# Local attention in pairs of 64 queries, values projected from the turned tokens, queries written three times and loaded in one transfer

## What is computed

```python
# allowed(i, j) = (j % 4 == 0) | (|i - j| <= 8);  16 heads of 8 features
x = x + 0.5 * ffn(layernorm(x))        # ffn: W_exp, butterfly, gelu, butterfly, W_con
x = x + attn(layernorm(x))
x = x + 0.5 * ffn(layernorm(x))

def attn(x):
    q, k, v = x @ q_w, x @ k_w, x @ v_w
    q = q * sigmoid(unity_scale)
    scores = where(allowed, q @ k.T / sqrt(8), -inf)
    return softmax(scores) @ v @ o_w + o_b
```

## Time and profile before

| | us |
|---|---|
| three runs | 346.88, 350.77, 351.96 |
| profiled execution, whole time | 348.5 |
| profiled execution, span from first to last instruction | 346.7 |
| PE busy | 278.6 |
| ACT busy | 201.4 |
| DVE busy | 160.1 |
| first score matmul | 114.5 |
| score matmuls of step 4 of the first unit | 128.0 |

### The profile page before, as it was taken

The page is one execution under the profiler, slowest core; times in us unless marked ns, Lnnn a source line. Parts: engine busy times, 40 slices in busy tenths (PEclk is TensorE's granted clock), DMA queues, the critical chain, the costliest instruction groups (busy, mean ns, idle before and its releaser), DMA issues.

```text
span 346.7 us, 5449 instructions
## 1 busy us (share of the span) xinstructions
PE 278.6 (80%) x2153; PEld 138.8 (40%) x2153; DVE 160.1 (46%) x421; ACT 201.4 (58%) x242; POOL 15.3 (4%) x15
## 2 busy tenths in 40 slices
PE   2299877893700429999899998999998999999995
PEld 0066673762400003233344434343443444347664
DVE  0799539899650001143425553255433544246410
ACT  1113335442410326799888998889998799952441
POOL 8000002102200000000000000000000000000000
PEclk9998989998565555899999999999999999999999
DMA  7900002326255530033312332123322300000111
GB/s 227 215 2 3 0 0 91 100 95 203 91 218 144 179 107 3 3 88 92 86 44 54 92 85 79 36 75 90 78 60 51 86 2 2 0 3 0 50 44 30
DMA packets 29242, 25.21 MB, mean 73 GB/s; under 512 B 4694, under 2 KB 25878, under 8 KB 29194
## 3 DMA queue, kind: packets, MB, share of 16 engines
q1 hardware_dynamic: 26501, 21.34, 22.1%
q10 hardware_dynamic: 2712, 3.49, 2.8%
HBM read 17.39 MB, written 7.63 MB: 72 GB/s over the span
## 4 chain that ended last, share of the span: by engine, by line
PE 68%; DVE 10%; SPq 9%; DMA 7%; ACT 2%; issue 1%; ACTq 1%; DVEq 0%
PE ps L585 19%; PE ps L566 18%; PE ps L459 8%; PE ps L418 6%; PE ps L572 5%; PE ps L595 5%; DMA k_strided<-k_strided_parts 3%; SPq L279 3%; PE ps L607 2%; DMA k_strided_parts<-probs_all 2%; DMA up_bias_sb<-L_ffn_up_bias 2%; DVE xnorm L822 2%; SPq L284 2%; PE ps L429 2%; SPq L307 2%
## 5 line engine op out<-in xcount | busy, mean ns | idle before, releaser
L762 ACT ACTIVATE probs_all<-ps 128x1024 f32<-128x1024 f32 x128 | 125.0, 1024 | 44.4 <-DMA q_parts<-probs_all 22.1
L566 PE MATMUL ps<-q_slots,k_strided 75*128 75x512 bf16 x256 | 74.0, 402 | 28.2 <-DMA v_local<-v_local_by_key 14.8
L585 PE MATMUL ps<-probs_all,v_strided 128*32 128x512 f32 x512 | 70.6, 625 | 0.0
L1019 DVE SCALAR_TENSOR_TENSOR probs_all<-probs_all,mask_k_sb 128x1024 f32<-128x1024 f32 x32 | 38.9, 1223 | 51.6 <-ACT probs_all L767 51.6
L566 PEld LDWEIGHTS ps<-q_slots,k_strided 75*128 75x128 bf16 x256 | 19.9, 100 | 86.3 <-ACT probs_all L762 28.5
L767 ACT ACTIVATE probs_all<-ps 128x1024 f32<-128x1024 f32 x32 | 32.7, 1021 | 9.2 <-PE ps L572 9.2
L691 ACT ACTIVATE gelu_h<-ps,bias_up 128x512 f32<-128x512 f32 x32 | 22.0, 687 | 24.7 <-PE ps L418 22.3
L418 PE MATMUL ps<-xnorm_t,up_folded 128*128 128x512 f32 x64 | 30.9, 627 | 3.4 <-ACT v_strided L717 1.9
L459 PE MATMUL ps<-down_folded,gelu_h 128*128 128x128 f32 x256 | 31.4, 283 | 2.1 <-ACT gelu_h L691 1.5
L459 PEld LDWEIGHTS ps<-down_folded,gelu_h 128*128 128x128 f32 x256 | 30.4, 198 | 3.6 <-ACT gelu_h L691 2.8
L992 DVE COPY o_sb<-ps 128x512 f32<-128x512 f32 x16 | 11.1, 691 | 39.9 <-PE ps L595 36.2
(11 more groups left out here) (90 smaller groups left out, 215.5 us busy)
## 6 DMA issues: line engine op xcount, KB each, us to landing
q_slots<-q_parts SPq DMA_DIRECT2D x48, 96.0 KB
k_local<-k_local_parts SPq DMA_DIRECT2D x48, 78.0 KB
v_local<-v_local_by_key SPq DMA_DIRECT2D x16, 216.0 KB
v_local_by_key<-v_block ACTq DMA_DIRECT2D x4, 768.0 KB, 7.2
q_parts<-probs_all SPq DMA_DIRECT2D x4, 384.0 KB, 4.2
k_local_parts<-probs_all SPq DMA_DIRECT2D x4, 288.0 KB, 4.1
k_strided<-k_strided_parts SPq DMA_DIRECT2D x4, 288.0 KB
out<-resid SPq DMA_DIRECT2D x4, 256.0 KB, 2.4
```

The lines of the kernel that those rows point to most:

```text
L566: mm = pe.matmul(PS[:, b0 + c, :], KS[:, ch, G * g + h, :], QS[:, g, h, :], start=True, stop=True)
L585: mm = pe.matmul(PS[VC * h:VC * (h + 1), 6, :], VS[:, 2 * pair + c, G * g + h, :], PE_[:, pair, h, c, :], start=(pair == 0 and c == 0), st ...
L762: act.activation(PE_[:, pair, h, :, :], PS[:, b0:b0 + 2, :], ACT.Exp).then_inc(p_ready, 1)
L1019: dve.scalar_tensor_tensor(pl, pl, 3.0e38, MK[:, None, :].to_broadcast([P, 2 * TB, P]), ALU.min, ALU.mult).then_inc(pl_ready, 1)
```

## The change

1. **Queries.** `q_parts` gets one more dimension, and each block's 384 KB are written three times (L300, 3 transfers). `load_q` is then a single transfer of 72 rows of 4 KB, with a source of 72 equal steps. `load_strided` becomes three transfers of 24 rows, also with equal steps. Each unit waits for 6 loads instead of 9.
2. **Values.** The strided and the local turned tokens are kept for all blocks (`XTS`, `XTL`). `qkv` projects the values of a window of 64 keys from `XTL` straight into the half of the partitions on which the attention needs them: one matmul for the strided ones and two per tile of 128 queries, over 3, 4, 4 and 5 tiles in blocks 0 to 3 (before, 4 matmuls). ACT copies them in one narrow and two wide copies (before, 128 and 384 columns; now 128 and twice 384 to 640) to where they stay. `VN`, the DRAM tensor `v_local_by_key`, its four writes and all `load_v` are gone.
3. **Local attention.** A query tile is two windows of 64 queries, one in each half of the partitions, each with its 64 keys (60 used). All four heads fit into one step: 32 matmuls of 64 columns by 64 queries, one exponential and one mask product of 128x1024 each. A unit has 9 steps.
4. **Outputs.** The values of both windows of a pair lie side by side in the 32 columns of a head: `values` makes 8 matmuls of 256 queries a call instead of 4 of 512; its two later calls stand together behind step 2; `values_local` has the same number of matmuls, of 64 queries each. The sum has 256 columns instead of 512: half the copy, 2 transposes instead of 4, and two multiplications by the reciprocal instead of one.
5. The tokens are handed over and given back in an order in which two windows of a pair lie in different tiles; `turn_rows` restores the natural order as it writes to PSUM.

```diff
-        q_st = nc.dram_tensor("q_parts", [NB, PARTS, P, QB], BF16, kind="Internal").ap()
+        q_st = nc.dram_tensor("q_parts", [NB, PARTS, PARTS, P, QB], BF16, kind="Internal").ap()
...
-                src = bass.AP(ks_st.tensor, ks_st.offset + b * PARTS * P * P,
-                              [[0, PARTS], [NH * P, PARTS * D], [1, NH * P]])
-                sp.dma_start(KS[0:PROD, b, :, :].rearrange("r h k -> r (h k)"), src).then_inc(ld_ks[b], 16)
+                for i in range(PARTS):
+                    sp.dma_start(KS[i * PARTS * D:(i + 1) * PARTS * D, b, :, :].rearrange("r h k -> r (h k)"),
+                                 ks_st[b].rearrange("j (d h) k -> (j d) (h k)", h=NH)).then_inc(ld_ks[b], 16)
...
-                for i in range(PARTS):
-                    src = bass.AP(q_st.tensor, q_st.offset + (it * PARTS + i) * P * QB + G * g * QB,
-                                  [[0, PARTS], [NH * QB, D], [1, G * QB]])
-                    rows = slice(i * PARTS * D, (i + 1) * PARTS * D)
-                    sp.dma_start(QS[rows, g, :, :].rearrange("r h s -> r (h s)"), src).then_inc(done, 16)
+                src = q_st[it].rearrange("i j (d h) s -> (i j d) h s", h=NH)[:, G * g:G * (g + 1), :]
+                sp.dma_start(QS[0:PROD, g, :, :], src).then_inc(done, 16)
...
-                sp.dma_start(q_st[b].rearrange("i p s -> p i s"), QKP[b % 2][:, :, 0:QB]).then_inc(q_out[b], 16)
+                for j in range(PARTS):
+                    sp.dma_start(q_st[b, :, j].rearrange("i p s -> p i s"), QKP[b % 2][:, :, 0:QB]).then_inc(q_out[b], 16)
...
-                for t in range(TB):
-                    mm = pe.matmul(PS[:, 3, t * P:(t + 1) * P], XTR[:, t * P:(t + 1) * P], VW[:, :], start=True, stop=True)
+                mm = pe.matmul(PS[:, 3, 0:P], XTS[:, b, :], VW[:, :], start=True, stop=True)
+                for n, t in enumerate(pairs_of(b), 1):
+                    for r in range(2):
+                        mm = pe.matmul(PS[r * W:(r + 1) * W, 3 + n // TB, n % TB * P:(n % TB + 1) * P],
+                                       XTL[:, (2 * t + r) * WSTEP:(2 * t + r) * WSTEP + W], VW[:, :], start=True, stop=True)
...
-                    for c in range(2):
-                        h = 2 * (s - 8) + c
+                    for h in range(G):
                         for t in range(TB):
-                            mm = pe.matmul(PS[:, b0 + c, t * P:(t + 1) * P], KL[:, g, h, t * TK:t * TK + P],
-                                           QS[:, g, h, t * P:(t + 1) * P], start=True, stop=True)
+                            for r in range(2):
+                                w = 2 * t + r
+                                mm = pe.matmul(PS[r * W:(r + 1) * W, b0 + h // 2, (h % 2 * TB + t) * W:(h % 2 * TB + t + 1) * W],
+                                               KL[:, g, h, w * WSTEP:w * WSTEP + W], QS[:, g, h, w * W:(w + 1) * W], start=True, stop=True)
...
-                for h in range(G):
-                    mm = pe.matmul(PS[VC * h:VC * (h + 1), 6, :], VS[:, 2 * pair + c, G * g + h, :], PE_[:, pair, h, c, :],
-                                   start=(pair == 0 and c == 0), stop=False, skip_group_check=True)
+                for r in range(2):
+                    for h in range(G):
+                        at = VSW * (G * g + h) + V1 * (1 - r)
+                        probs = PE_[:, pair, h, c, :].rearrange("p (t r q) -> p r t q", t=TB, r=2)[:, r]
+                        mm = pe.matmul(PS[VC * h:VC * (h + 1), 6, 0:QB // 2], VS[:, 2 * pair + c, at:at + VC], probs,
+                                       start=(pair == 0 and c == 0 and r == 0), stop=False, skip_group_check=True)
...
-                        if before and s == 1:
+                        if before and s == 2:
                             values(*before, 1, 0)
-                        if before and s == 2:
                             values(*before, 1, 1)
...
-                        if s == 8:
+                        if s == 7:
                             values(it, g, 0, 1)
```

More of the change, by code:

```diff
@@ L36 @@
 DNN = 24 + 2 ** STAGES * 2 - 8
[L37 removed]
+SLOT_LOADS = PARTS + 3
 W = 64
@@ L43 @@
 TK = 3 * P // 4
-TWIN = TK + 2 * PADK
 BW = (TB - 1) * TK + P
 VC = 32
+V1 = D + 1
+VSW = 3 * V1
+VLW = 2 * V1
+XLW = 3 * S // 4 + 16
 BIG = -1.0e30
@@ L111, in program @@
         SOF, LOF = QB, QB + P
[L112 to L114 removed]
+        VS = sb("v_strided", [P, NCH, NH * VSW + VC - VLW])
+        VL = sb("v_local", [P, NT, NH * VLW + VC - VLW])
         ZB = sb("zerosb", [P, LK - PADK - 3 * S // 4], BF16)
@@ L187, in program @@
         pl_ready = sem("pl_ready")
-        v_out = [sem(f"v_out{b}") for b in range(NB)]
         sig = sem("sig")
@@ L231, in program, with pairs_of @@
         UPB = [WUP[:, 0:2 * NC]] + levels(4 * NC, 0)
+        def pairs_of(b):
+            return range(max(0, TB * b - 1), TB * b + TB - (b < NB - 1))
         DNB = [WDN[:, 0:2 * NC]] + levels(4 * NC, 2 * NC * HID)
@@ L358, in _ @@
             for b in range(NB):
-                sp.wait_ge(q_out[b], 16)
-            for b in range(NB):
-                sp.wait_ge(v_out[b], 16)
+                sp.wait_ge(q_out[b], 16 * PARTS)
             for it in range(1, NB):
@@ L602, in turn @@
                 if n:
-                    pe.wait_ge(o_ctx, n)
+                    pe.wait_ge(o_ctx, 2 * n)
                 if g == 0 and it:
                     pe.wait_ge(x2_done, it)
-                for t in range(TB):
+                for t in range(2):
                     mm = pe.transpose(PS[:, 7, t * P:(t + 1) * P], OS[:, t * P:(t + 1) * P], ID[:, :])
@@ L712, in qkv @@
                 act.wait_ge(qkv_ps, 3 * b + 3)
-                if b >= 2:
-                    act.wait_ge(v_out[b - 2], 16)
-                act.activation(VN[:, b % 2, :, :, 0:D], PS[:, 3, P:QB].rearrange("p (t h d) -> p t h d", t=3, d=D),
-                               ACT.Copy).then_inc(v_ready, 1)
-                act.activation(VS[:, b, :, 0:D], PS[:, 3, 0:P].rearrange("p (h d) -> p h d", d=D),
-                               ACT.Copy).then_inc(v_ready, 1)
-                act.wait_ge(v_ready, 2 * b + 1)
-                act.dma_start(v_st[PADK + 3 * P * b:PADK + 3 * P * (b + 1), :].rearrange("(t p) c -> p t c", p=P),
-                              VN[:, b % 2].rearrange("p t h c -> p t (h c)")).then_inc(v_out[b], 16)
+                vps = PS[:, 3:5, :].rearrange("p a b -> p (a b)")
+                n = len(pairs_of(b))
+                act.activation(VS[:, b, 0:NH * VSW].rearrange("p (h k) -> p h k", h=NH)[:, :, V1:V1 + D],
+                               vps[:, 0:P].rearrange("p (h d) -> p h d", d=D), ACT.Copy).then_inc(v_ready, 1)
+                for r in range(2):
+                    rows, ts = slice(r * W, (r + 1) * W), slice(pairs_of(b)[0], pairs_of(b)[0] + n)
+                    act.activation(VL[rows, ts, 0:NH * VLW].rearrange("p t (h k) -> p t h k", h=NH)[:, :, :, r * V1:r * V1 + D],
+                                   vps[rows, P:(n + 1) * P].rearrange("p (t h d) -> p t h d", t=n, d=D), ACT.Copy).then_inc(v_ready, 1)
             act.wait_ge(sig, 3)
@@ L998, in finish_unit @@
                     dve.wait_ge(ct_ps, it)
-                dve.tensor_tensor(CT[:, :, G * D * g:G * D * (g + 1)].rearrange("p t (h d) -> p t h d", h=G),
-                                  ov[:, :, :, 0:D], RD[:, :, :, None].to_broadcast([P, TB, G, D]),
-                                  ALU.mult).then_inc(o_ctx, 1)
+                for r in range(2):
+                    dve.tensor_tensor(CT[:, r:TB:2, G * D * g:G * D * (g + 1)].rearrange("p t (h d) -> p t h d", h=G),
+                                      ov[:, :, :, r * V1:r * V1 + D], RD[:, :, :, r:r + 1].to_broadcast([P, 2, G, D]),
+                                      ALU.mult).then_inc(o_ctx, 1)
             def finish_block(it):
@@ L1015, in mask_local @@
                 n = NG * it + g
[L1016 to L1020 removed]
+                dve.wait_ge(p_ready, NSTEP * n + 9)
+                edge = 0 if it == 0 else 2 if it == NB - 1 else 1
+                band = MK[:, edge:edge + TB, :].rearrange("p t q -> p (t q)")[:, None, :].to_broadcast([P, G, TB * W])
+                pl = PL[:, :, :, :].rearrange("p h t q -> p h (t q)")
+                dve.scalar_tensor_tensor(pl, pl, 3.0e38, band, ALU.min, ALU.mult).then_inc(pl_ready, 1)
             for it in range(NB):
@@ L1056, in constants @@
     far = np.abs(rel[:, None] - q[None, :]) > LOCAL
-    keys = np.arange(P)
-    relt = STRIDE * (keys // 3) + keys % 3 + 1 - LOCAL
-    mask_k = np.where(np.abs(relt[:, None] - keys[None, :]) <= LOCAL, 1.0, 0.0)
+    inside = np.abs(np.concatenate([rel, np.full(W - WIN, BIG)])[:, None] - q[None, :]) <= LOCAL
+    mask_k = np.zeros((2, W, TB + 2, W), np.float32)
+    for t in range(TB + 2):
+        for w in range(2):
+            key = (0 if t == 0 else NT - 1 if t == TB + 1 else 1) * P + w * W + np.concatenate([rel, np.zeros(W - WIN)])
```

(3 more changed lines are left out.)

116 lines of the change are left out of this document (52 added, 64 removed).

## The result

The kernel after takes 315.69 us (median of 4 runs, 314.08 to 317.81), the one before 350.94 (346.88 to 351.96, 4 runs): ratio 0.902, 95% interval 0.893 to 0.911. The forecast was 323, its range 314 to 336. On the chips of the experiments the kernel before took 343.5 to 350.2 us in its fast executions and 350.7 to 352.8 in its slow ones, so that a ratio, which is of fast ones alone, can move by a per cent from chip to chip.

The account below looks back on a forecast made before the run. Slow query loads filling SP's queue were taken to bound the start-up, PE the attention. From 348.5 us: start-up -19.7, values' copies +0.2, four blocks -6.0, last unit -0.4 give 322.6, called 323; range 314 to 336.

Parts of the forecast that it names:

- signs of being wrong: Issues of several us in SP's queue, a local step over 1.3 or under 0.7 us, values over 1.1 a call.
- The bound read from SP's queue and the DMA share: Start-up: query loads with outermost dimension 3 use few DMA engines (23% busy, 89 GB/s), filling SP's queue and starving PE.
- Start-up: Ahead of the attention: faster loads let step 4's scores start at 108.3 instead of 128.02, -19.7 us (-17 to -22).
- The clock: PE after step 4: another 13 us at the lower level as before, nothing counted; up at once, 6.5 us as bound.
- Values' copies: ACT's wider copies in the projection: 0.8 us more a block, mostly hidden behind PE's wait for DVE, counted +0.2 us.
- Local scores: Attention unit: 32 matmuls with 64 weight columns, two side by side, taken at 1.0 us (bounds 0.55 and 1.8), no gain.
- Local values: Attention unit: half the columns, as many instructions, 0.8 us instead of 1.01, so -0.2 us.
- the wait: Attention, step 2's scores wait for the local step's exponential: about 0.3 us in two of a block's four units.
- small matmuls cheap, or the clock back early: Rival, attention and start: local scores and values 0.6 us each, or clock up to 6.5; 313 us, chance 0.19.
- transfers no faster: Rival, start-up: loads stay at 89 GB/s, SP stuck as before, only the attention gains; 342 us, chance 0.10.
- the dear matmuls: Rival, attention: each of 32 local scores costs a full one's 56 ns, step 1.8 us; 336 us, chance 0.15.
- the slower case: Rival, attention: 64-column weight loads hide behind nothing, local scores 4.0 us a unit, +48; 371 us, chance 0.03.

Follow-up runs that it names:

- The run with the old patterns: Kernel after with queries written once and sources with an outermost dimension of 3, all else changed: 325.23 us, 0.943 of the kernel before.
- without the branch: Kernel after without the three conditional blocks behind the bounds flag (the fallback, not run on this input): 315.59 us, 0.908 of the kernel before.
- the run with the transfers alone: Kernel before with part 1 of the change only (queries written three times, loads with equal steps): 330.28 us, 0.957 of the kernel before.

## Why the prediction was right, and where it wasn't

The time came within the range, and the bound in the start-up was the one named. That it came within 8 us of the forecast is in part luck: the attention gained 11.8 us more than forecast, and the start-up, with the slower stages ahead, 5.6 less. One of the signs of being wrong did show, a local step under 0.7 us.

- **The bound read from SP's queue and the DMA share: right.** Share, issues and block 3's write came out as said (0.4 us late beyond the shift of 2.7). The run with the old patterns shows the cause: with values dropped the share stays 0.23.
- **Start-up, forecast -19.7 (-17 to -22): measured -16.6.** The step that failed is the path: "PE's conditions for its first scores (queries, strided keys 0 and 1, the flag)" leave out the conditional block behind the flag, which held PE for 7 us and stood in no row that I had read. Before, it was hidden: PE's first scores came 14 us behind the flag for the loads' sake. The runs divide the 3.1 us. Behind block 3's first write step 4 came 12.4 us later, forecast 9.7; without the branch it is 10.7. So in these executions 1.7 are the conditional block's, 1.0 the transfers', and 0.4 the later split. The first part of the transfers' sum was nearly right: without the branch the query parts had landed 7.3 us behind that write (forecast 6.7).
- **The clock, forecast "I count nothing": wrong by some 4 us between the profiled executions.** I took the 13 us of the trace before for a property of the start; in the run with the transfers alone, with the same attention, the clock rose 5.0 behind step 4. After, PE worked 9.6 us at half speed from its first scores, 6.2 of them behind step 4. It was in the sum as a bound ("up to 6.5"), and should have had weight. Other executions of before spent up to 12.5 us less at half clock than the profiled one, so part of the 4 us is the draw of that execution. The reading of the slices had a slip here too: PE wasn't idle in all of slices 10 to 15, but busy for seven and nine tenths of the first and the last.
- **Values' copies, +0.2: right in the mechanism.** `ffn_up` waits 1.51 and 1.75 us for them, forecast 1.7 from 0.95, and the split of block 3 is 0.4 late in all.
- **Joined `values` (1.86) and transposes (0.22): right**, each to 0.03.
- **Local scores, forecast 1.0: measured 0.65. Local values 0.8: 0.58.** The row nearest in kind, weight loads with a short matmul each in 1.01 for 32, had longer matmuls, and I didn't take off for them. These two terms are mis-sized by 0.57 a unit; the wait came out smaller as well, forecast 0.3 and measured 0.15. A unit got 0.82 to 0.87 shorter, not 0.5 less the wait.
- **Two slips in the sums.** Four times 0.5 less twice 0.3 is 1.4 a block, 5.6 in four, where the forecast has 6.0. And SP is through with the queries by 87 to 92 by the terms given, not 88.7 to 93.7. Neither moves the forecast by more than 0.4.
- **The block's last two units**, -1.24 and -1.38. In the second, the chain before held DVE's copy and the transposes behind it, 1.43 us from 177.10 to 178.53; after, the copy of half the columns (0.42 us instead of 0.69) hides behind two score matmuls and 0.44 of transposes stay. I had counted the transposes and not the wait that ends with them.

```profile
155.63 0.58 PE ps L596 x32
156.21 0.54 PE ps L562 x2
156.75 0.01 issue
156.76 0.44 PE ps L608 x2
```

- Together the attention gave 18.2 (14.1, 3.7 in its first unit, which the clock shares, and 0.5 behind the last), where I had 6.4; the start-up, its +0.2 included, gave 2.9 less. With the 2.7 of the stages ahead that is 322.6 - 11.8 + 2.9 + 2.7 = 316.4, and 316.7 was measured: the rest lies outside the span. The rival "small matmuls cheap, or the clock back early" (313) was what happened in the attention, "forecast" what happened ahead of it. Of the other rivals, transfers no faster (342) fell with the share of 0.80, the dear matmuls and the slower case (336, 371) with the 16 ns that one more costs.

## What to carry to other kernels

When the DMA share is low and the queue's issues are long, look at the outermost dimension of the source: here writing the queries three times was 10 to 15 us cheaper than repeating them in the pattern (9.8 us of start-up with the values dropped, 14.8 with them there). Price a small matmul by its own columns, not by the nearest row of larger ones, and follow a halved tile to the copy and the wait behind it. Behind a large gain at a stage's start, look for the limit just beneath, which may be nothing that a semaphore shows, such as a branch. Before a term is read off one profiled execution, compare its mean granted clock with that of the other runs.

## What the runs showed of the hardware

- While loads were under way whose source repeats by an outermost dimension of 3, the DMA engines moved 87 to 89 GB/s at a share of 0.23, with issues of 3 to 5 us in the queue behind them; with equal steps, and more writes beside them, 227 to 251 GB/s at 0.80 to 0.87, issues of such loads 0.4 us.
- In the nine kernels with the conditional block where no load came last, PE's first scores stood 6.1 to 8.0 us behind the flag's last instruction, beside busy transfers; in the two without it, 0.2 us. (In the run with the old patterns it was 8.5, and the last thing PE waited for was a load of local keys.)
- 32 matmuls of 64 weight columns by 64 queries, two side by side in the array, took 0.65 us, and 32 more only 0.52, 16 ns each, the weight load of each included. The Trainium skill ("TensorE: Matmul & The Clock Gate", section "Wait — 56ns, not 53.3ns?") gives a floor of about 25 ns between starts; this chain goes below it.
- Behind step 4 PE, busy throughout, stayed at 1.2 GHz for 13.6 us in the profiled execution of before and for 5.0 to 7.1 in the twelve others. The idle time ahead of step 4 doesn't explain it: 7.3 us before, but also 6.6 in the run with the old patterns, which stayed there for 6.8. What does stays open. And an idle time of 1.2 us in otherwise full work was followed, in six cases of 21, by 3.4 us at half speed.
